# Two-layer MetaFormer with routed experts: who makes image 1's normalised rows for layer 1 (ScalarE or VectorE), and where their store stands

## What is computed

```python
def _L1_ffn_ref(x, gate_w, gate_b, w1, b1, w2, b2):   # x: (2, 4096 tokens, 128)
    gate_logits = flat_x @ gate_w + gate_b
    raw_weights = jax.nn.softmax(gate_logits, axis=-1)
    top_w, top_idx = jax.lax.top_k(raw_weights, TOP_K)             # 2 of 8 experts
    h = jax.nn.gelu(jnp.einsum('td,edh->teh', flat_x, w1) + b1, approximate=False)
    expert_out = jnp.einsum('teh,ehd->ted', h, w2) + b2
    combined = jnp.einsum('ted,te->td', expert_out, gate_output)
# with x = _from_tokens(t, x); x = x + _L1_conv_ref(_ln_c(x), ...)
# t = _to_tokens(x);  t = t + _L1_ffn_ref(_ln_t(t), ...)
```

## Time and profile before

| | |
|---|---|
| median of 3 runs | 989.05 us (987.12 to 992.66) |
| span of the profiled execution | 1121.3 us; no other time of that execution is on hand |
| PE, DVE, ACT, POOL busy | 72%, 50%, 46%, 55% of the span |
| POOL indirect transfers | 284 gathers and 284 scatters |
| chain that ended last | PE 40%, DVE 26%, ACT 10%, an unknown releaser 10%, issue 8% |

### The profile page before, as it was taken

One profiled execution on the slowest core, in us unless ns is written; L12 is line 12 of the kernel. 1 busy time (PEld: TensorE's weight loads), 2 busy tenths in 40 slices (PEclk: granted clock), 3 DMA queues, 4 the chain that ended last, 5 costly groups with the idle time before them and its releaser, 6 DMA issues.

```text
span 1121.3 us, 14549 instructions
## 1 busy us (share of the span) xinstructions
PE 810.7 (72%) x4233; PEld 683.7 (61%) x4233; DVE 565.6 (50%) x1308; ACT 516.3 (46%) x1407; POOL 616.5 (55%) x590
## 2 busy tenths in 40 slices
PE   1854389897867867986689488975996677796780
PEld 0434268785767655864678376854786565674670
DVE  8957902280500291999775296999681003300005
ACT  1405045562444445653266156643393443453563
POOL 1000266676655675788623755888646466665640
PEclk9876579997988888998589689998798788998895
DMA  8001344453565742553137733543256446555456
GB/s 317 1 0 57 123 149 125 139 156 98 174 193 187 248 156 87 172 158 118 38 109 236 254 110 109 183 138 102 65 162 220 135 128 201 194 157 174 133 162 225
DMA packets 54557, 165.23 MB, mean 147 GB/s; under 512 B 13632, under 2 KB 13645, under 8 KB 54224
## 3 DMA queue, kind: packets, MB, share of 16 engines
q1 hardware_dynamic: 36304, 128.87, 34.6%
q0 software_dynamic: 18176, 35.44, 10.8%
HBM read 134.89 MB, written 31.20 MB: 148 GB/s over the span
## 4 chain that ended last, share of the span: by engine, by line
PE 40%; DVE 26%; ACT 10%; another core or an unknown queue 10%; issue 8%; DMA 3%; POOL 2%; SPq 0%; POOLq 0%; ACTq 0%; DVEq 0%
PE h_ps L783 14%; PE yT_ps L796 12%; DVE state L1302 6%; DVE work L1288 4%; DVE work L1283 4%; ACT hT L596 4%; PE turn_ps L718 4%; PE acc_ps L735 3%; DVE tok L1252 2%; PE acc_ps L755 2%; DVE work L1296 2%; PE xT_ps L772 2%; ACT yT L607 1%; PE h_ps L886 1%
## 5 line engine op out<-in xcount | busy, mean ns | idle before, releaser
L511 POOL DMA_INDIRECT xg<-xn_rows,tile_rows x284 | 305.4, 1075 | 243.1 <-DVEq L1218 126.6
L520 POOL DMA_INDIRECT y_rows<-yr,tile_rows x284 | 306.9, 1080 | 236.1 <-ACT yr L616 147.5
L783 PE MATMUL h_ps<-xT,expert 128*128 128x256 f32 (+1 forms) x1376 | 317.7, 381 | 64.9 <-ACT hT L596 37.7
L796 PE MATMUL yT_ps<-hT,expert 128*128 128x256 f32 (+1 forms) x1376 | 300.2, 369 | 34.9 <-ACT yT L607 21.6
L596 ACT ACTIVATE hT<-h_ps,expert 128x256 f32<-128x256 f32 (+1 forms) x688 | 250.7, 451 | 154.7 <-PE h_ps L783 70.0
L783 PEld LDWEIGHTS h_ps<-xT,expert 128*128 128x128 f32 x1376 | 244.4, 213 | 103.1 <-issue 52.6
L796 PEld LDWEIGHTS yT_ps<-hT,expert 128*128 128x128 f32 x1376 | 247.5, 209 | 71.6 <-ACT yT L607 26.1
L1252 DVE SCALAR_TENSOR_TENSOR tok<-work,share,tok 128x128 f32<-128x128 f32 x224 | 61.2, 346 | 340.3 <-DMA work<-y_rows 336.9
L607 ACT ACTIVATE yT<-yT_ps,expert 128x256 f32<-128x256 f32 (+1 forms) x172 | 72.9, 444 | 170.3 <-PE yT_ps L796 92.4
L584 ACT ACTIVATE xT<-xT_ps 128x256 f32<-128x256 f32 x144 | 56.4, 392 | 117.8 <-PE xT_ps L772 59.7
L772 PE MATMUL xT_ps<-ident,xg 128*128 128x128 f32 x284 | 61.2, 298 | 58.2 <-DMA xg<-xn_rows,tile_rows 45.4
(11 more groups left out here) (210 smaller groups left out, 661.1 us busy)
## 6 DMA issues: line engine op xcount, KB each, us to landing
expert<-in_experts SPq DMA_DIRECT2D x172, 514.5 KB
work<-y_rows SPq DMA_DIRECT2D x24, 512.0 KB
xn_rows<-work SPq DMA_DIRECT2D x16, 512.0 KB, 4.4
xg<-xn_rows,tile_rows POOLq DMA_INDIRECT x284
y_rows<-yr,tile_rows POOLq DMA_INDIRECT x284
tok<-in_x_tokens SPq DMA_DIRECT2D x8, 512.0 KB, 6.9
state<-in_x SPq DMA_DIRECT2D x2, 2048.0 KB, 17.1
work<-y_rows SPq DMA_DIRECT2D x16, 256.0 KB, 6.1
```

What stands on the lines that cost most here:

```text
L511: pool.indirect_dma_start(xg[:, s, h, :], None, xn_rows[unit], bass.IndirectOffsetOnAxis(ap=tile_rows[unit % 2][:, at, 0, h:h + 1], axis=0)) \
L520: pool.indirect_dma_start(y_rows[unit], bass.IndirectOffsetOnAxis(ap=tile_rows[unit % 2][:, at, 1, h:h + 1], axis=0), yr[:, s, h, :], None ...
L783: mm = pe.matmul(h_ps[c // 2][:, c % 2, cols], expert[:, t.load(h) % W_RING, c * P:(c + 1) * P], xT[:, t.slot(2), cols], start=True, stop= ...
L796: mm = pe.matmul(yT_ps[:, cols], expert[:, t.load(h, d) % W_RING, HIDDEN + c * P:HIDDEN + (c + 1) * P], hT[:, s, c, cols], start=(c == 0), ...
```

## The change

For image 1 in layer 1 the ScalarE instructions go (no entry "route_rows" is left for unit 3), VectorE makes the rows after `route(3)`'s shares with the code it had for unit 1 (the condition `u == 1` becomes `b == 1`), and the store's entry moves from step 30 (`rows[-1]`) to 34. For image 0 (unit 2) nothing moves: its store was at 33 and is given as 33.

```diff
-def mixing(b, read, state, norm, route, slots, rows, invert):
+def mixing(b, read, state, norm, route, slots, rows, invert, store):
...
-    steps += [(rows[q], "route_rows", u, q) for q in range(QUARTERS)]
+    steps += [(at, "route_rows", u, q) for q, at in enumerate(rows)]
...
-    return steps + [(rows[-1], "route_store", u)]
+    return steps + [(store, "route_store", u)]
...
-    mixing(1, read=2, state=(4, 5, 5.6, 6), norm=7, route=(25, 25.6), slots=28, rows=(27.3, 28.6, 29.3, 30),
-           invert=(30.3, 30.6, 31, 31.3)),
+    mixing(1, read=2, state=(4, 5, 5.6, 6), norm=7, route=(25, 25.6), slots=28, rows=(),
+           invert=(30.3, 30.6, 31, 31.3), store=34),
...
-                if u == 1:
-                    dve.wait_ge(s_xn_st[0], 16 * QUARTERS)
+                if b == 1:
+                    dve.wait_ge(s_xn_st[u - 1], 16 * QUARTERS)
                     for q in range(QUARTERS):
                         for t in range(BLOCKS)[quarter(q)]:
                             ins = dve.tensor_scalar(work_tok[0][:, t, :], tok[b][:, t, :], mean[:, t:t + 1],
```

More of the change, by code:

```diff
@@ L88 @@
     mixing(0, read=3, state=(6, 7, 7.6, 8), norm=11, route=(28, 28.3), slots=30.3, rows=(30, 31, 31.6, 33),
-           invert=(33, 33.3, 34, 34.3)),
-    mixing(1, read=2, state=(4, 5, 5.6, 6), norm=7, route=(25, 25.6), slots=28, rows=(27.3, 28.6, 29.3, 30),
-           invert=(30.3, 30.6, 31, 31.3)),
+           invert=(33, 33.3, 34, 34.3), store=33),
+    mixing(1, read=2, state=(4, 5, 5.6, 6), norm=7, route=(25, 25.6), slots=28, rows=(),
+           invert=(30.3, 30.6, 31, 31.3), store=34),
     [(8, "outputs", 2, 0), (10, "outputs", 2, 1), (12, "outputs", 2, 2), (14, "outputs", 2, 3),
```

## The result

The changed kernel took 1011.09 us (median of 4, 1007.04 to 1016.88) against 990.86 us (median of 4, 987.12 to 992.71) for the kernel before. The ratio is 1.0214, 95% interval 1.0171 to 1.0256: slower by 21 us, where the prediction had 13.8. The direction came as forecast, and so did the gate that carries the loss to the end. The size was two thirds of the measured one, and the price of the store's place, which the prediction put at nothing, was not.

What follows compares the result with a forecast made beforehand. No engine bounds the whole; in unit 3 POOL is slower than PE, 203 us for 157 transfers. Its first gather moving from 846.3 to 860.1 adds 13.8 to 989.05: 1003 us, own range 999 to 1009, wider range 996 to 1012.

Steps and rivals of the forecast that it cites:

- The gate and what lies behind it: Handover to unit 3: the row store holds POOL's first gather; any delay there delays the end one for one.
- The reading of the first profile's waits without a releaser: ScalarE's 69.8 us at the gelu and similar waits: mostly a product of the profiled execution; timed runs 132 us shorter.
- PE sets the pace: Rival, unit 3: PE rather than POOL sets the pace, so the loss is PE's, +10.2 us, 999 us; chance 0.14.
- Not slower, hidden: Rival, unit 3: existing stalls hide the late gate, leaving only PE's 2.4 us gain, 986.7 us; chance 0.11.
- SP comes late: Rival, step 34: SP issues the stores only from 868, behind a stall; gate at 880, +20, 1009 us; chance 0.13.
- The signs named ahead: Handover: shares within 3 us, L1235 8 to 9 us, POOL idle about 25, PE waiting some 10, no L634 at 812 to 835.
- VectorE's term: After the row lists: shares 3.46 us, then 32 row instructions 8.47 us, 12.1 us between row lists and last quarter.
- The landing: Store's last quarter, after four stores and two weight loads: lands 5.5 us after issue, with ends 2.6 and 8.6.
- So SP's place costs nothing: Step 34 in SP's queue: SP arrives at about 853, before the last quarter at 854.1, so no cost.
- ScalarE's relief: Steps 27 to 30: without ScalarE's 32 instructions the row lists come at 842.0, a gain of 2.7 us.
- The sum: Unit 3's first gather moves from 846.3 to 860.1, +13.8 us (ends +10.3 and +19.6), giving 1003 us.
- the wider range, to 1012: Whole kernel: the forecast's range, plus PE's pace down to 996 and half of SP late up to 1012.

Runs made afterwards that it cites:

- the store at 31: The changed kernel with VectorE's rows ahead of the shares and unit 3's store at step 31: median 1006.04 us, ratio 1.0128.

## Why the prediction was right and wrong

**The gate and what lies behind it: right.** That POOL, blocked at unit 3's first gather, sets the end one for one is shown twice: 225.9 to 226.7 us from gate to end in the first seven profiles of the table, with POOL's order unchanged and gates from 760.7 to 784.9 (227.0 and 228.4 in two more), and 8 scatters moved ahead of it take 10 us off. The reading of the first profile's waits without a releaser as a product of that execution was right as well: two later spans are 986.7 and 993.3.

**The rivals.** *PE sets the pace* is out: POOL has hardly a gap in unit 3 beyond 0.3 us. *Not slower, hidden* is out. *SP comes late* is out as it was written: there is no stall, and SP was at the store 10.4 us after the lists, about where the forecast had it (853 against 842, 11 us). What neither it nor the forecast had is that SP's place costs as much as the whole change even then, as the kernel shows in which only the store moved.

**The signs named ahead.** The 32 L1235 rows, the missing L634 and the late gate are there. POOL's idle time grew by 26 us, not by 14, and PE waited 14.9 us instead of 10: the gate came later, and POOL had also stopped earlier, its last transfer ending 14 us ahead of the lists. It lost nothing by that, since it could not go on before the gate.

**VectorE's term: right.** Shares and rows took 761.3 to 773.2, 11.9 us for a forecast of 12.1, the rows 8.29 for 8.47. The 4.1 us that the Trainium skill's formula gave (VectorE: DVE Perf Modes, the TRN2 errata) differ from this measurement too.

**The landing: mis-sized.** The step that failed reads "With 1.5 MB of stores and 1 MB of weights ahead, some 7 us of work at that rate of which half is done by then, I take 5.5". The last store left at 773.8, 0.6 us after its rows, took 9.5 us, and POOL began 0.7 us later: the gate 10.8 us behind the rows instead of 6.0. The half that was to be done by then was not: 2.7 us after the last issue at least 1.6 MB were left, the engines had moved 256 GB/s since 771.6 and not 342, and two more loads joined. The burst of the kernel before, behind two loads as well, had its last landing after 8.6 us, and after 8.6 and 7.5 in the later profiles: the 5.5 lay under all three.

The sentence ahead of it, "So SP's place costs nothing", failed with it. SP came 1.5 us before the last quarter was made (forecast: 1.1), so three stores went out in one burst with the fourth close behind, all of them behind two weight loads issued in the 1.5 us before. The error was to treat SP's place as costless because SP arrived just before the last rows. Moved alone it costs the whole 21 us, and taken from 34 back to 32 it gives 6.8 us at the gate. The rows' 12 us and SP's 10 us overlap; the burst's 9 us come on top of either, and an SP that waits at the store for each quarter avoids most of them (2.6 to 3.0 us with the store at 32).

**ScalarE's relief: mis-sized.** 2.7 us forecast; 1.4 us in the traces, nothing measurable alone. The forecast had PE take up the third one-hot block as soon as it was ready; in the changed kernel it was ready at 751.68, and PE, still on the second, took it up at 752.58.

**The sum.** Lists to gate 22.6 instead of 0.7 (means of two profiles each), +21.9, less 1.4 of relief: 20.5 us, against a measured 2.14% of 991, 21.2 us. The forecast's 13.8 was 18.1 for the new way from lists to gate, less 1.6 for the old and 2.7 of relief. Of the 6.7 us between 13.8 and 20.5 the new way, all of it in the landing, is 4.5, the old way 0.9 and the relief 1.3. The forecast's own range (999 to 1009) missed the median of 1011 by its upper end, whose landing was bounded at 8.6 us by a burst of stores with fewer weights ahead. That the wider range, to 1012, holds it is luck: its upper end was there for half of *SP late*, whose stall did not come.

## What to carry to other kernels

Where a table sets the order on a queue, a store's place has two prices: when the queue gets there, and how much is issued in one burst around it when it does. Work that gates another engine's next phase should stand where its queue waits for it, not where it waits for its queue. And an engine that sits idle at a gate, with work of its own queued behind the gate, should do that work first; but only the part whose inputs are there before the gate opens.

## What the runs showed of the hardware

The same 512 KB store from SBUF to HBM landed in 2.6 to 3.0 us when four were issued about 2 us apart amid tile work with no weight load in the 3.8 us before (the store at 32), in 4.9 to 6.5 us when four were issued 1.4 to 2.1 us apart behind two weight loads (the store at 33), and in 6.5 to 9.5 us when four were issued within 2.1 us behind two weight loads, at 330 GB/s and 89% DMA share (the changed kernel). With the store at 31 and no weight load in the 8 us before, stores 2 us apart took 2.9 to 4.5 us; what these waited for the runs don't show.

POOL's first gather of unit 3 started 0.75 or 0.76 us after the last store's landing in all eleven profiles in which the store was what it waited for.

One profiled execution of the kernel before was 135 and 128 us longer than two later ones; ScalarE waited there without a releaser for 69.8 us at the gelu, 68.0 at the bias and 37.0 at the copy of the turned rows, and in the later ones not at all.

After a wait of 7 to 9 us 32 small multiplies of PE took 4.0 us in one execution and 6.8 in another, of kernels that are alike up to there, at a mean granted clock of 0.71 and 0.64 over the 24 us around them.
